# A per-image mixed 3x3 convolution on one core: reordered first loads, small steps moved between mixture shares, and joined stores in the last pair

## What is computed

```python
pooled = x.mean(axis=(2, 3))
a = relu(einsum('bc,kc->bk', pooled, fc1_w) + fc1_b)
att = softmax(einsum('bk,jk->bj', a, fc2_w) + fc2_b, axis=1)
agg_w = einsum('bk,koihw->boihw', att, weight)
agg_b = att @ bias
out = x + conv(gn(x), agg_w) + agg_b      # x of the conv and of the pooling is gn(x)
```

## Time and profile before

| | us |
|---|---|
| median of 3 runs | 313.08 |
| the three runs | 312.87, 313.08, 314.52 |
| profiled execution, its own time | 314.18 |
| its span, first to last instruction | 312.3 |
| TensorE busy in it | 297.9 |
| VectorE busy in it | 246.5 |
| ScalarE busy in it | 189.8 |

### The profile page before, as it was taken

How to read it: one execution, slowest core, us unless ns; L and a number is a source line. 1 busy time by engine, 2 the same in 40 slices (tenths; PEclk the granted TensorE clock), 3 DMA queues, 4 the chain that set the end, 5 groups by cost and what they waited for, 6 DMA issues and landing times.

```text
span 312.3 us, 15651 instructions
## 1 busy us (share of the span) xinstructions
PE 297.9 (95%) x7029; PEld 266.2 (85%) x7029; DVE 246.5 (79%) x760; ACT 189.8 (61%) x241; POOL 22.9 (7%) x32
## 2 busy tenths in 40 slices
PE   7299998999999999999999999999999999999994
PEld 5256866778787989999987998899999999999993
DVE  2988897888999998999798989889696987856000
ACT  1292937739194676738386868767684866767321
POOL 1004040040400000000000000000000000000000
PEclk9779999999999999999999999999999999999999
DMA  7893084480946658482936869495664416070564
GB/s 254 329 395 108 2 266 150 121 290 13 279 139 221 197 171 245 135 250 58 295 106 185 233 161 238 128 240 176 173 188 136 135 35 178 2 195 18 144 171 105
DMA packets 19283, 53.62 MB, mean 172 GB/s; under 512 B 7568, under 2 KB 10896, under 8 KB 19216
## 3 DMA queue, kind: packets, MB, share of 16 engines
q1 hardware_dynamic: 18912, 52.41, 56.6%
q10 hardware_dynamic: 304, 0.22, 0.3%
HBM read 26.89 MB, written 25.69 MB: 168 GB/s over the span
## 4 chain that ended last, share of the span: by engine, by line
PE 75%; DVE 10%; ACT 8%; issue 3%; DMA 2%; SPq 0%; DVEq 0%; ACTq 0%
PE acc L793 75%; DVE stats L324 2%; ACT o L675 2%; DMA x<-x 2%; DVE mix L436 2%; ACT xh L623 2%; ACT x L605 2%; ACT wh L653 1%; DVE xl L512 1%; ACT xh L631 1%; ACT wh L640 0%; DVE wparts L343 0%; DVE x L520 0%; DVE mix L434 0%; DVE mv L332 0%
## 5 line engine op out<-in xcount | busy, mean ns | idle before, releaser
L793 PE MATMUL acc<-xh,wh 64*64 64x385 f16 (+3 forms) x2304 | 112.1, 326 | 1.3 <-ACT xh L623 0.7
L793 PE MATMUL acc<-xl,wh 64*64 64x385 f16 (+3 forms) x2304 | 111.1, 325 | 0.6 <-issue 0.4
L793 PE MATMUL acc<-xh,wl 64*64 64x385 f16 (+3 forms) x2304 | 110.6, 325 | 0.6 <-issue 0.6
L675 ACT ACTIVATE o<-acc,out_par 128x392 f32<-128x392 f32 x127 | 78.2, 669 | 52.9 <-PE acc L793 52.7
L793 PEld LDWEIGHTS acc<-xh,wh 64*64 64x64 f16 x2304 | 87.8, 107 | 12.0 <-ACT wh L653 1.6
L793 PEld LDWEIGHTS acc<-xl,wh 64*64 64x64 f16 x2304 | 90.9, 107 | 7.7 <-issue 1.3
L793 PEld LDWEIGHTS acc<-xh,wl 64*64 64x64 f16 x2304 | 87.8, 107 | 10.2 <-issue 1.0
L324 DVE BATCH_NORM_STATS2 stats<-x 128x6 f32<-128x448 f32 x112 | 64.9, 615 | 5.2 <-DMA x<-x 5.2
L631 ACT ACTIVATE xh<-x,xof,xsc 128x1568 f16<-128x1568 f32 x24 | 40.5, 1690 | 32.3 <-DVE xof L398 32.3
L512 DVE TENSOR_TENSOR xl<-x,xh 128x1568 f16<-128x1568 f32 x28 | 49.9, 1785 | 8.1 <-ACT x L605 7.9
L436 DVE SCALAR_TENSOR_TENSOR mix<-w_sb,ex,mix 128x192 f32<-128x192 f32 (+1 forms) x72 | 44.2, 614 | 0.9
(11 more groups left out here) (60 smaller groups left out, 135.6 us busy)
## 6 DMA issues: line engine op xcount, KB each, us to landing
x<-x SPq DMA_DIRECT2D x30, 784.0 KB, 6.5
out<-o SPq DMA_DIRECT2D x30, 392.0 KB, 5.0
out<-o SPq DMA_DIRECT2D x30, 294.0 KB, 4.6
out<-o SPq DMA_DIRECT2D x44, 98.0 KB, 3.5
out_par<-par SPq DMA_DIRECT2D x64, 0.5 KB, 2.0
x<-x SPq DMA_DIRECT2D x2, 448.0 KB, 4.9
x<-x SPq DMA_DIRECT2D x3, 224.0 KB, 6.2
w_sb<-w_t SPq DMA_DIRECT2D x2, 288.0 KB, 4.9
```

The costliest lines, as they stand in the source:

```text
L675: nc.scalar.activation(o_sb[i][m][:, g * GN:(g + 1) * GN], acc[n % SLOTS][m][:, 0:GN], ACT.Identity, bias=out_par[i][m][:, 1:2], scale=out ...
L793: ins = nc.tensor.matmul(pixels[:, top:bottom, left:right], weights[i][halves[m], tap * C:(tap + 1) * C], window, start=start and step == ...
```

## The change

x0 comes in four pieces of two, two, two and one chunks, and the weights are issued behind the landing of the third. The sum of exponentials and the weight scale become steps between the shares (`scale_step`), and the bias product has a semaphore of its own, so that `params_step` has three steps in place of four. ScalarE makes the first quarter of `xh` ahead of the exponentials in pairs 1 to 3. There are 54, 10, 10, 6, 6 and 4 constant products, some behind new waits on TensorE. In pair 15 the two DMAs of an image's group become one, whose destination is a view [2 bands, 64 channels, 392 pixels] and whose source is 128 partitions by 392 pixels: 8 DMAs in place of 16.

```diff
-PIECES = ((0, 1), (1, 3), (3, 5), (5, 6), (6, 7))
+PIECES = ((0, 2), (2, 4), (4, 6), (6, 7))
-WARM_PRODUCTS = (36, 6, 9)
+WARM_PRODUCTS = (54, 10, 10, 6, 6, 4)
+        def group_of(p, g, m):
+
+            bands = out_d[2 * p + m].rearrange("c (b n) -> b c n", n=GN)
+            upper, lower = BANDS[0][g], GROUPS + BANDS[1][g]
+            return bands[upper:lower + 1:lower - upper], o_sb[p % 2][m][:, g * GN:(g + 1) * GN]
...
                 for m in range(2):
                     sp.wait_ge(s_res, 2 * GROUPS * p + 2 * g + m + 1)
-                    for r in range(2):
-                        first = r * HALF + BANDS[r][g] * GN
-                        sp.dma_start(out_d[2 * p + m, :, first:first + GN],
-                                     o_sb[i][m][halves[r], g * GN:(g + 1) * GN]).then_inc(stored[i][m], 16)
+                    sp.dma_start(*group_of(p, g, m)).then_inc(stored[p % 2][m], 16)
...
-            sp.wait_ge(x_piece[1], 16)
+            sp.wait_ge(x_piece[2], 16)
...
+            sp.dma_start(*group_of(last_pair, g, 0)).then_inc(stored[i][0], 16)
...
-                    total = 48 * pairs if i != last_pair % 2 else 48 * (pairs - 1) + 32 * GROUPS
+                    total = 48 * pairs if i != last_pair % 2 else 48 * (pairs - 1) + 16 * GROUPS
...
+            def scale_step(p, k):
+
                 n, i = LINKS * p, p % 2
+                if k == 0:
+                    nc.vector.tensor_reduce(exsum[:], ex[:], AX.X, ALU.add).then_inc(dch, 1)
+                elif k == 1:
+                    dve.wait_ge(dch, n + 3)
+                    nc.vector.scalar_tensor_tensor(out=stdx[:], in0=std[i][:], scalar=WLIMIT, in1=exsum[:],
+                                                   op0=ALU.mult, op1=ALU.mult).then_inc(dch, 1)
+                    total = tiny[i][:, RANGE:RANGE + 1]
+                    if p == 0:
+                        dve.wait_ge(s_range, 1)
+                        nc.vector.scalar_tensor_tensor(
+                            out=wrange[:], in0=tiny[0][:, WEIGHTS:WEIGHTS + 1], scalar=total, in1=exsum[:],
+                            op0=ALU.add, op1=ALU.mult).then_inc(dch, 1)
+                    else:
+                        nc.vector.tensor_scalar(wrange[:], total, exsum[:], None, ALU.mult).then_inc(dch, 1)
+                elif k == 2:
+                    dve.wait_ge(dch, n + 5)
+                    nc.vector.reciprocal(wsc[i][:], wrange[:]).then_inc(s_wsc, 1)
...
-                exponential_sum(p)
-                weight_scale(p)
                 done = shares(p)
                 for k in range(K):
                     share(p, k, slice(0, TAPS * C), done + k)
+                    scale_step(p, k)
                     params_step(p, k)
...
-                        if n == 1:
+                        if n == 0:
+                            scale_step(p, k)
+                        elif n == 1:
                             params_step(p, k)
...
-                    nc.vector.reciprocal(rsum[:], exsum[:]).then_inc(dch, 1)
+                    nc.vector.tensor_tensor(bprod[:], ex[:], small_sb[:, BIAS:BIAS + K], ALU.mult).then_inc(s_bias, 1)
                 elif k == 1:
-                    nc.vector.tensor_tensor(bprod[:], ex[:], small_sb[:, BIAS:BIAS + K], ALU.mult).then_inc(dch, 1)
+                    nc.vector.reciprocal(rsum[:], exsum[:])
+                    dve.wait_ge(s_bias, 2 * p + 1)
+                    nc.vector.tensor_reduce(bsum[:], bprod[:], AX.X, ALU.add).then_inc(s_bias, 1)
                 elif k == 2:
-                    dve.wait_ge(dch, n + 7)
...
+                    dve.wait_ge(s_bias, 2 * p + 2)
...
             for p in range(1, EARLY):
                 results(p - 1, 0)
-                results(p - 1, 1, (0,))
+                high_quarter(p, 0)
                 exponentials(p)
-                results(p - 1, 1, (1,))
-                high_quarter(p, 0)
+                results(p - 1, 1)
                 high_quarter(p, 2)
...
-                    for r in range(2):
-                        first = r * HALF + BANDS[r][GROUPS - 1] * GN
-                        act.dma_start(out_d[2 * p + 1, :, first:first + GN],
-                                      o_sb[p % 2][1][halves[r], HALF - GN:HALF]).then_inc(stored[p % 2][1], 16)
+                    act.dma_start(*group_of(p, GROUPS - 1, 1)).then_inc(stored[p % 2][1], 16)
...
-            keep_warm(WARM_PRODUCTS[0])
+            keep_warm(0)
+            pe.wait_ge(s_stats, 1)
+            keep_warm(1)
             image_sums(0)
-            keep_warm(WARM_PRODUCTS[1])
+            keep_warm(2)
             first_range()
-            keep_warm(WARM_PRODUCTS[2])
+            keep_warm(3)
+            pe.wait_ge(s_exp, 1)
+            keep_warm(4)
+
+            pe.wait_ge(s_part, K - 1)
+            keep_warm(5)
```

More of the change, by code:

```diff
@@ L169, in dynamic_conv @@
         s_share = sem("s_share")
+        s_bias = sem("s_bias")
         s_mix = sem("s_mix")
@@ L225, in store_group @@
             def store_group(p, g):
-                i = p % 2
                 for m in range(2):
                     sp.wait_ge(s_res, 2 * GROUPS * p + 2 * g + m + 1)
-                    for r in range(2):
-                        first = r * HALF + BANDS[r][g] * GN
-                        sp.dma_start(out_d[2 * p + m, :, first:first + GN],
-                                     o_sb[i][m][halves[r], g * GN:(g + 1) * GN]).then_inc(stored[i][m], 16)
+                    sp.dma_start(*group_of(p, g, m)).then_inc(stored[p % 2][m], 16)
             for n, (first, last) in enumerate(PIECES):
@@ L258, in _ @@
             sp.wait_ge(s_res, 2 * GROUPS * PAIRS - 1)
-            for r in range(2):
-                first = r * HALF + BANDS[r][g] * GN
-                sp.dma_start(out_d[2 * last_pair, :, first:first + GN],
-                             o_sb[i][0][halves[r], g * GN:(g + 1) * GN]).then_inc(stored[i][0], 16)
+            sp.dma_start(*group_of(last_pair, g, 0)).then_inc(stored[i][0], 16)
             for i in range(2):
@@ L308, in _ @@
         def _(dve):
-            LINKS = 8
+            LINKS = 5
             def link(n, ins):
@@ L408, in logits @@
                 nc.vector.tensor_reduce(nmax[:], logit[:], AX.X, ALU.max, negate=True).then_inc(s_logit, 1)
-            def exponential_sum(p):
+            def scale_step(p, k):
                 n, i = LINKS * p, p % 2
[L412 to L426, removed]
+                if k == 0:
[15 more added lines that the diff above has]
+                    nc.vector.reciprocal(wsc[i][:], wrange[:]).then_inc(s_wsc, 1)
             def share(p, k, part, done):
@@ L462, in mixture_in_parts @@
                     dve.wait_ge(s_wh, mixed(p - 1))
-                exponential_sum(p)
-                if p >= 1:
-                    weight_scale(p)
                 for n, part in enumerate(PARTS):
@@ L478, in mixture_in_parts @@
                             share(p, k, part, done + k)
-                        if n == 1:
+                        if n == 0:
+                            scale_step(p, k)
+                        elif n == 1:
                             params_step(p, k)
                     if n == 0:
-                        if p == 0:
-                            weight_scale(p)
                         dve.wait_ge(s_part, done + K)
@@ L534, in params_step @@
                         nc.vector.tensor_scalar(par[i][:, 0:1], total, 1.0 / XSCALE, None, ALU.mult)
-                    nc.vector.reciprocal(rsum[:], exsum[:]).then_inc(dch, 1)
+                    nc.vector.tensor_tensor(bprod[:], ex[:], small_sb[:, BIAS:BIAS + K], ALU.mult).then_inc(s_bias, 1)
                 elif k == 1:
-                    nc.vector.tensor_tensor(bprod[:], ex[:], small_sb[:, BIAS:BIAS + K], ALU.mult).then_inc(dch, 1)
+                    nc.vector.reciprocal(rsum[:], exsum[:])
+                    dve.wait_ge(s_bias, 2 * p + 1)
+                    nc.vector.tensor_reduce(bsum[:], bprod[:], AX.X, ALU.add).then_inc(s_bias, 1)
                 elif k == 2:
-                    dve.wait_ge(dch, n + 7)
-                    nc.vector.tensor_reduce(bsum[:], bprod[:], AX.X, ALU.add).then_inc(dch, 1)
-                else:
-                    dve.wait_ge(dch, n + 8)
+                    dve.wait_ge(s_bias, 2 * p + 2)
                     nc.vector.tensor_scalar(par[i][:, 1:2], bsum[:], rsum[:], gm[i][:], ALU.mult,
@@ L771, in first_range, with keep_warm @@
                                  start=True, stop=True).then_inc(s_range, 1)
-            def keep_warm(products):
-                for _ in range(products):
+            def keep_warm(n):
+                for _ in range(WARM_PRODUCTS[n]):
                     nc.tensor.matmul(acc[SLOTS - 1][0][:, 0:2 * P], ones[:].bitcast(fp16)[:, 0:P],
```

## The result

The changed kernel takes 337.04 us (median of 4 runs, 336.12 to 338.56), the kernel before beside it 313.37 us (4 runs): a ratio of 1.076, 95% interval 1.072 to 1.080, so 23.7 us slower. The forecast was 333.4 us, with 324.5 to 347.0 as its range. The profiled execution took 336.12 us with a span of 334.3.

What follows compares the result with a forecast made beforehand. TensorE was taken as the bound, busy 297.9 of 312.3 us. Gains 1.4 + 0.35 + 1.0 = 2.75 us start the stores' data at 294.1; + 1.9 + 35.8 + 0.8 = 332.6, median 333.4 us, range 324.5 to 347.

Steps and rivals of the forecast that it cites:

- Two engines for a joined store: Pair 15's output stores: each joined DMA is carried by two of the 16 DMA engines, bounds two and sixteen; chance 0.81.
- Price of a row: Pair 15's joined stores: 70 ns per 1568-byte row, bounds 57 and 100; eight stores of 64 rows per engine, 35.8 us.
- The start of the backlog: End of the run: first issue 295.84 − 2.75, data 1.0 later at 294.1, behind 1.9 us of pair 14's stores.
- The step from the profiled execution to the median: Whole run: the median stands 1.10 us below the profiled execution, so 334.5 becomes 333.4 us.
- Loads: Start: x0's statistics end 1.5 us sooner, less 0.1 us waiting for weights; net gain 1.4 us, bounds −0.3 and 1.9.
- Small steps: Pair 0: sum of exponentials, its product and weight scale moved between the shares save 0.35 us, bounds 0.1 and 0.49.
- Clock, ScalarE's order and pair 4: Pairs 1, 3 and 4: products come 0.4, 0.3 and 0.3 us sooner, together 1.0, bounds 0 and 2.0, clock's gain included.
- Stores saving 0.4 us: End of the run: half of two issues saved, 0.4 us, bounds 0 and 0.6, if joined stores move like today's.
- The signs named: DMA share near 0.12 from 300 us, fewer completions, joined landings over 20 us, SyncE's last wait near 20, start clock 1.00.

## Why the prediction was right, step by step

- **Two engines for a joined store**: right, and shown: the completions (14 for 7 stores), the DMA share of 0.13, and the same loss from 62 plain rows. The argument from counts, that each old transfer ended once on sixteen engines, gave the tool by which the engines of any transfer can be counted. The rule of the Trainium skill, "DMA: Bandwidth & Descriptors", section "Why a DMA increments its semaphore by 16 and not by 1", holds for 2, 62, 57 and 61 too. The rows before, without that rule, had left the case open.
- **Price of a row**: 70 ns assumed. In the tail of the changed kernel it is 1568 bytes at 23 GB/s, 68 ns. Eight stores of 64 rows are 34.9 us (35.8 forecast). The low bound's side was right. Counted as in the earlier trace rows, by the packets' own time, a row took 73 ns (13.5% of 16 engines for 357 packets in the 12 us from 320 on) where it took 93 to 100 ns with sixteen engines at work; that competition makes the difference was the prediction's reason and is not shown by itself.
- **The start of the backlog**: the first joined store was issued at 293.99, 1.85 us sooner than 295.84, not 2.75. 293.99 + 1.0 + 34.9 = 329.9, and the data end near 333.3, so backlog and gaps were 3.4 us, not 1.9 (from 297 to 299 only 19 and 24 GB/s moved). These two misses, and 1.0 us rather than 0.8 from the last data to the end of the span, would make 2.6 us; the price of a row took 0.9 back, so the span was 334.3 where the forecast was 332.6. That errors of both signs met is luck.
- **The step from the profiled execution to the median**: I took 1.10 us off, as the profiled execution of before stood above its median. The changed kernel's profiled execution was its fastest of four, 0.9 below its median. That is 2.0 of the 3.6 us between 333.4 and 337.04.
- **Loads**: gain 1.4 forecast, 1.2 against this one trace of before, but 0.7 on the mean of traces. The term was mis-sized because the trace of before had the latest statistics of the six old-order traces (10.00; the others 8.45 to 9.38). The weights landed in time, as assumed: issued at 7.13, awaited by SyncE until 9.92.
- **Small steps**: 0.35 forecast, 0.15 measured in pair 0: what was late next was ScalarE with its two shares, which I had not looked for.
- **Clock, ScalarE's order and pair 4**: 1.0 forecast together, 1.1 measured. From the first product to the products behind the last quarter of `xh` in pair 1 it is 21.77 us before and 21.23 after, 0.54 less (0.4 forecast); from the start of the group to the start of the next it is 5.13 and 4.81 in pair 3, 0.32 less (0.3), and 1.89 and 1.65 in pair 4, 0.24 less (0.3). In pair 1 the experiments give 0.25 to ScalarE's order, 0.19 to the small steps, to which the prediction gave nothing there, and 0.13 to the constant products. Up to the last read-out only 0.6 us is left of it (290.04 us from the first product before, 289.41 after): the changed trace has 1.7 us of pauses, that of before 1.0.
- **Stores saving 0.4 us**: never seen, since no joined store went to 16 engines.
- **The signs named**: the share, the completions and the clock came as named. The landings were not shown for joined stores, and SyncE's last wait was 12.5 us, not 20: it was held at the issue of the stores before, up to 8.2 us for one.

## What to carry to other kernels

Before joining DMAs, look at the outermost dimension of both sides: a view with two bands, images or halves in front puts the whole transfer on two engines, and 62 or 61 rows are as bad as 2 or 1. Count the completions in a queue's packets to see how many engines each transfer used. Two issues took 1.11 and 1.25 us, so one issue less is worth about 0.6 us at most, and no run here showed even that; compare it with rows times 68 ns over the engines that are left.

A tuned kernel's small gains need several traces of each side: here the start of one and the same stream varied by 1.5 us, as much as the change brought there (17.97 to 16.58 for the first product). Where an engine pauses for nothing that the profile names, look for a transfer of instructions that ended just before the pause did.

## What the runs showed of the hardware that was not expected

- A DMA engine moved rows of 1568 bytes at 22.5 to 23 GB/s, whether one, two or three of the sixteen carried the tail's load.
- The issue of a transfer blocks its engine's stream when the few DMA engines are behind: the six joined stores on SyncE took 0.87 to 8.2 us to issue, where the earlier trace rows has 12 issues in 11.6 us that mostly wait for results.
- Stores can slow TensorE though it awaits none of them: with the early stores cut, its pauses went from 2.0 us to none and the last read-out from 305.92 to 303.53 in these two traces; the medians differ by 1.1 us. Each of the 29 pauses ended 1.25 to 1.58 us behind a 16 KB transfer of instructions.
